# Interleaving the relation matches with the edge selections on VectorE in a four-layer graph kernel

## The reference, cut to what matters

```python
def rgcn_conv(x, edge_index, edge_type, W, root, bias):
    out = x @ root + bias
    for r in range(8):
        mask = edge_type == r
        h = x @ W[r]
        msg = jnp.where(mask[:, None], h[src], 0)
        agg = segment_sum(msg, dst)
        cnt = segment_sum(mask, dst)
        out = out + agg / jnp.maximum(cnt, 1.0)[:, None]
    return out
# x = x + relu(conv3(relu(conv2(relu(conv1(relu(layernorm(x))))))))
# x = x + batchnorm_mlp(h + segment_sum(h[src], dst)),  h = relu(layernorm(x))
```

## Time and profile before

| | |
|---|---|
| median of 3 runs | 2309.25 us (2307.88 to 2319.2) |
| the profiled execution | 2311.88 us, of which its span is 2309.9 us |
| busy in the span | POOL 1660.0 us (72%), PE 1422.0 us (62%), DVE 711.2 us (31%), ACT 99.0 us (4%) |
| DMA | 186.42 MB moved, mean 81 GB/s |

### The profile page before, as it was taken

One profiled execution on the slowest core, in us unless ns is written; L12 is line 12 of the kernel. 1 busy time (PEld: TensorE's weight loads), 2 busy tenths in 40 slices (PEclk: granted clock), 3 DMA queues, 4 the chain that ended last, 5 costly groups with the idle time before them and its releaser, 6 DMA issues.

```text
span 2309.9 us, 13665 instructions
## 1 busy us (share of the span) xinstructions
PE 1422.0 (62%) x4287; PEld 1023.7 (44%) x4287; DVE 711.2 (31%) x2460; ACT 99.0 (4%) x182; POOL 1660.0 (72%) x1671
## 2 busy tenths in 40 slices
PE   4646465564675667667676656656655566566566
PEld 2334344343453445545454444444444355444445
DVE  4675655656522122222212122122122111111111
ACT  2100000000000000000000000000000000000001
POOL 0387777777776777777775777777776777777774
PEclk9755555555555555555555555555555555555555
DMA  6533333333322223223222122222221211222222
GB/s 205 194 106 102 122 121 104 119 103 121 118 75 65 59 83 89 63 80 89 66 84 79 53 57 57 53 56 58 52 57 51 53 53 53 53 53 53 53 53 62
DMA packets 94459, 186.42 MB, mean 81 GB/s; under 512 B 31010, under 2 KB 45229, under 8 KB 91053
## 3 DMA queue, kind: packets, MB, share of 16 engines
q0 software_dynamic: 53248, 109.16, 18.4%
q1 hardware_dynamic: 41132, 76.33, 9.4%
HBM read 142.59 MB, written 42.77 MB: 80 GB/s over the span
## 4 chain that ended last, share of the span: by engine, by line
POOL 70%; issue 22%; PE 4%; DMA 1%; DVE 1%; ACT 0%; SPq 0%; POOLq 0%; DVEq 0%; ACTq 0%
POOL rows L627 70%; PE ps_h L294 3%; PE ps_agg L320 1%; DMA rows<-h_table,idx 0%; DMA x_rows<-in_x 0%; DMA h_table<-stage 0%; DVE xr_rows L438 0%; DVE ln_stat L425 0%; DVE stage L368 0%; SPq L551 0%; DMA rows<-xr_table,src_i 0%; ACT sel L697 0%; PE ps_agg L965 0%; DVE ln_mv L429 0%; DVE small L736 0%
## 5 line engine op out<-in xcount | busy, mean ns | idle before, releaser
L320 PE MATMUL ps_agg<-sel,rows 128*128 128x64 f32 (+15 forms) x3776 | 1137.0, 424 | 814.4 <-DMA rows<-h_table,idx 615.2
L627 POOL DMA_INDIRECT rows<-h_table,idx x1248 | 1262.9, 1012 | 490.4 <-issue 379.4
L320 PEld LDWEIGHTS ps_agg<-sel,rows 128*128 128x128 f32 x3776 | 922.0, 314 | 1169.9 <-DMA rows<-h_table,idx 733.6
L468 DVE TENSOR_SCALAR sel<-iota,dst_f,norm 128x64 f32<-128x64 f32 x1248 | 295.6, 334 | 793.1 <-PE ps_agg L320 792.2
L627 POOL DMA_INDIRECT rows<-xr_table,src_i x416 | 393.0, 945 | 134.6 <-issue 126.5
L294 PE MATMUL ps_h<-w_all,xT 128*128 128x512 f32 x300 | 239.5, 919 | 10.1 <-ACT stage L368 6.8
L470 DVE TENSOR_SCALAR sel<-iota,dst_f 128x64 f32<-128x64 f32 x416 | 75.3, 274 | 406.9 <-PE ps_agg L320 406.9
L368 DVE COPY stage<-ps_h 128x512 f32<-128x512 f32 x75 | 51.5, 687 | 265.9 <-PE ps_h L294 258.5
L453 DVE TENSOR_REDUCE count<-match 128x8 f32<-128x2048 bf16 x52 | 118.9, 2286 | 1.8
L449 DVE TENSOR_SCALAR match<-chunks,key_f 128x256 bf16<-128x256 f32 x416 | 114.1, 344 | 0.0
L294 PEld LDWEIGHTS ps_h<-w_all,xT 128*128 128x128 f32 x300 | 72.7, 282 | 38.8 <-issue 28.6
(11 more groups left out here) (67 smaller groups left out, 180.5 us busy)
## 6 DMA issues: line engine op xcount, KB each, us to landing
h_table<-stage SPq DMA_DIRECT2D x150, 256.0 KB, 2.4
chunks<-key_rows SPq DMA_DIRECT2D x26, 1088.0 KB, 6.0
rows<-h_table,idx POOLq DMA_INDIRECT x1248, 2.5
rows<-xr_table,src_i POOLq DMA_INDIRECT x416, 2.5
x_rows<-in_x SPq DMA_DIRECT2D x6, 256.0 KB, 5.3
w_all<-in_W SPq DMA_DIRECT2D x3, 512.0 KB, 4.2
out<-xr_rows SPq DMA_DIRECT2D x6, 256.0 KB
xr_table<-xr_rows SPq DMA_DIRECT2D x5, 256.0 KB, 2.3
```

What stands on the lines that cost most here:

```text
L320: mm = nc.tensor.matmul(sums_of(L, k)[:, at:at + width], rows[:, G % SLOTS, :], sel[:, G % SELS, in_window:in_window + width], start=False ...
L468: done = nc.vector.tensor_scalar(mine, here, dst, norm[:, t:t + 1], ALU.is_equal, ALU.mult)
L627: pool.indirect_dma_start(rows[:, slot, :], None, table, bass.IndirectOffsetOnAxis(ap=column, axis=0)).then_inc(landed, 16)
```

## The change: what it does

`count_batch` is split into `match_tile` (one match) and `norm_batch` (reduction and reciprocal), and `select` now makes one selection. In layer 0 the match of tile t+8 is issued right after the selection of tile t: one selection, one match, one selection, and so on, with the reduction and the reciprocal behind the eight pairs. The batch's signal to PE comes with the eighth selection as before; the signal `s_match` with the eighth match. Batch 0's matches still stand in a row. The number, shapes and operands of all instructions stay as they are.

```diff
-        def count_batch(dve, g):
-            c = BATCH * g // CHUNK
-            if BATCH * g % CHUNK == 0:
+        def match_tile(dve, t):
+            c, at = t // CHUNK, P * (t % CHUNK)
+            if t % CHUNK == 0:
                 dve.wait_ge(s_chunk[c % 2], 16 * (c // 2 + 1))
-            for n in range(BATCH):
-                at = P * (BATCH * g % CHUNK + n)
-                done = nc.vector.tensor_scalar(match[:, n, :], chunks[:, c % 2, at:at + 2 * P],
-                                               key_f[:, BATCH * g + n:BATCH * g + n + 1], None, ALU.is_equal)
-            done.then_inc(s_match, 1)
+            done = nc.vector.tensor_scalar(match[:, t % BATCH, :], chunks[:, c % 2, at:at + 2 * P], key_f[:, t:t + 1],
+                                           None, ALU.is_equal)
+            if t % BATCH == BATCH - 1:
+                done.then_inc(s_match, 1)
+
+        def norm_batch(dve, g):
             dve.wait_ge(s_match, g + 1)
             nc.vector.reduce_sum(count[:, g % 2, :], match[:], AXIS_X).then_inc(s_count, 1)
...
-        def select(dve, L, g):
+        def select(dve, L, t):
+            G = TILES * L + t
+            if t % BATCH == 0:
+                if G >= SELS:
+                    dve.wait_ge(s_mm, (G - SELS) // BATCH + 1)
+                if L == 0:
+                    dve.wait_ge(s_norm, t // BATCH + 1)
...
+            if t % BATCH == BATCH - 1:
+                done.then_inc(s_sel, 1)
...
                         if L == 0 and g == 0:
-                            count_batch(dve, 0)
-                        select(dve, L, g)
+                            for t in range(BATCH):
+                                match_tile(dve, t)
+                            norm_batch(dve, 0)
+                        for t in range(BATCH * g, BATCH * g + BATCH):
+                            select(dve, L, t)
+                            if L == 0 and t + BATCH < TILES:
+                                match_tile(dve, t + BATCH)
                         if L == 0 and g + 1 < TILES // BATCH:
-                            count_batch(dve, g + 1)
+                            norm_batch(dve, g + 1)
```

More of the change, by code:

```diff
@@ L455, in count_batch @@
             nc.vector.reciprocal(norm[:, BATCH * g:BATCH * g + BATCH], count[:, g % 2, :]).then_inc(s_norm, 1)
-        def select(dve, L, g):
[L459 to L471, removed]
+        def select(dve, L, t):
[5 more added lines that the diff above has]
+                    dve.wait_ge(s_norm, t // BATCH + 1)
+            mine, dst = sel[:, G % SELS, :], dst_f[:, t:t + 1]
+            here = iota[:, EARLY + start_of[t]:EARLY + start_of[t] + SPAN]
+            if L < GIN:
+                done = nc.vector.tensor_scalar(mine, here, dst, norm[:, t:t + 1], ALU.is_equal, ALU.mult)
+            else:
+                done = nc.vector.tensor_scalar(mine, here, dst, None, ALU.is_equal)
+            if t % BATCH == BATCH - 1:
+                done.then_inc(s_sel, 1)
         def close_residual(dve, k):
```

## The result

The changed kernel takes 2229.03 us (median of 4 runs, 2227.89 to 2231.01) against 2310.13 us of the kernel before on the same chip (4 runs): ratio 0.9643, 95% interval 0.9616 to 0.9670. It is faster by 81.1 us, where 51 were predicted. On the 2309.25 us shown ahead, the ratio gives 2226.8 us, 1.2 us under the low end of the range; the direction was right, the size was not.

What follows compares the result with a forecast made beforehand. POOL's rate of issuing gathers was taken as the bound. Of 81.6 us lost in layer 0, 32 would remain, gaining about 50: 2309.25 - 50 = 2259, stated as 2258 us, range 2228 to 2302.

Steps and rivals of the forecast that it cites:

- What bounds the kernel, and where the loss was: POOL issuing gathers makes up 92% of the span; layer 0's runs of matches lengthen its gathers by 81.6 us.
- That selections between matches let POOL in: In layer 0's pairs POOL gets in when a match ends, in 0.146 us with only a selection; gain about 50 us.
- The rival that a selection would hold the port as well: In layer 0, selection and match together keep POOL out: 92 us more, 2401 us; chance of slower 0.10.
- What remains: Layer 0's gathers still wait on single matches, 0.24 us a gather, 0.62 us a batch, 32 us over 51 batches.
- The rival of no change: Every layer 0 match costs POOL 0.20 us wherever it stands, so time stays at 2309 us; chance 0.12.
- POOL on DVE: Gathers delay layer 0's matches by at most 1.6 us a batch, hidden by DVE's waiting for PE.
- chunks: The wait for loads in layer 0 comes 1.6 us earlier; cost nothing, at most 40 us if uncovered.
- s_sel: The selections' signal to PE in layer 0 moves 1.8 us later, covered by PE's 35 us distance.
- the end of layer 0: POOL's 12.56 us wait for the table after layer 0's last gather shifts as a whole; PE can follow 50 us faster.

Runs made afterwards that it cites:

- e3_row_waits: The kernel before with its row of eight matches kept, but each match waits for the end of the one ahead; 2241.11 us.

## Why the prediction missed

**What bounds the kernel, and where the loss was:** right. The chain is POOL's, the loss was 81.6 us in layer 0, and it came from matches in a row; the recovery is 81.35.

**That selections between matches let POOL in:** right in effect. The rival that a selection would hold the port as well and so close the pairs did not come true: the longest gather behind batch 0 took 1.05 us. By the Trainium skill ("SBUF — State Buffer", "Who interferes with whom", with "Mode 2×_2P" of "VectorE: DVE Perf Modes") a selection fits the mode that holds the port. The traces agree with that only for a selection's last moments, as in the gather of 321.37 in `e3_row_waits` (1.02 us).

**The step that failed is "What remains":** "each of a gather's two moments falls inside a match with a chance 0.341 / 0.487 = 0.70, and then waits half a match, 0.17 us", 32 us in all. It took the exclusion, which the rows showed for a row of matches, for a property of each match over its whole 0.341 us. Measured, the remainder is 0.3 us. The count was right: 0.70 of 133 gathers is 93, and 90 first moments fell inside a match. The wait was wrong. A match with a selection behind it was open to all 77 gathers that came 0.12 to 0.20 us after its start (that of 309.40 is one) and is closed in its last 0.14 us (the gather of 113.25); with another match right behind it, it is closed till that one ends. The even spread of the gathers was wrong as well, and this was luck: only four of the 90 came in a match's last 0.14 us. The first error is the larger, since an even spread would have cost 3 to 12 us by the estimate above, not 32. Without that term the same sum is 2309.25 - 81.6 = 2227.7. The lower bound of the range was that very figure, and I gave it as an end although the term it stood for was a guess about something that no row showed.

**The rival of no change** was wrong: a match does not cost POOL its 0.20 us wherever it stands. The stall went with the matches' neighbours.

**POOL on DVE, chunks, `s_sel`, the end of layer 0:** right. The waits for chunks stayed at 0.0, PE's wait for selections 0.6 us, the wait for the table 12.21 us.

## What to carry to other kernels

Where GpSimd issues DMAs and is the bound, look for long issues, set their ends against VectorE's instructions, and count how many of the same wide single-input instructions stand in a row ahead of each end. Break such a row before you take work out of it: cut each instruction to 128 columns, or put another short one between two (here a memset or a 64-column selection did), and measure the leftover instead of charging it by a chance of overlap. It depends on where the ends of the issues fall, so it can differ from kernel to kernel. VectorE may even get more work by this, if it waits anyway.

## What the runs showed of the hardware that I had not expected

- The exclusion depends on the instruction behind: 256 columns in a row, 0.263 us apart, closed (81.6 us); with a 0.06 us memset between, 0.27 us apart, open (2.6 us).
- It depends on width, with the jump between 128 and 192 columns: stall 0.6, 1.1, 60.4 and 81.6 us at 64, 128, 192 and 256 columns, although starts are closer at 128 columns (0.20 us, as eight last 1.67 us) than at 256. With a second scalar operand 256 columns leave 11.9 us.
- It works both ways at no cost in POOL: matches beside gathers lasted up to 0.57 us, DVE giving way.
- A match that no other match overlaps is open to a gather 0.12 to 0.20 us after its start (77 gathers of the changed kernel, none over 0.96 us) and closed in its last 0.14 us (104 of 112 gathers of `e3_row_waits` waited there). Earlier than 0.12 us the runs differ (0.04 us lost for each gather in the changed kernel, 0.19 in `e3_row_waits`).
- How the port is handed over, and so why a match behind a match closes the time that a memset or a selection leaves open, stays open.
